# A mixture stage's routing: 64 squares on ACT for four subtractions on POOL, and the shares' operations at an earlier place

## The reference

```python
gate_logits = jnp.einsum('ble,en->bln', x, gate_kernel)
top_k_weights, top_k_indices = jax.lax.top_k(gate_logits, TOP_K)
softmax_probs = jax.nn.softmax(top_k_weights.astype(jnp.float32), axis=-1)
weights = weights.at[b_idx, l_idx, top_k_indices].set(softmax_probs)
layer_w0 = jnp.einsum('ble,neh->blnh', x, w0_kernel)
layer_w1 = jnp.einsum('ble,neh->blnh', x, w1_kernel)
layer_mult = jax.nn.silu(layer_w0) * layer_w1
intermediate = jnp.einsum('blnh,nhe->blne', layer_mult, wo_kernel)
output = jnp.einsum('blne,bln->ble', intermediate, weights)
```

## Time and profile before

| | before |
|---|---|
| median of 3 runs | 2676.36 us |
| the profiled execution: its time | 2678.13 us |
| the profiled execution: its span | 2676.4 us |
| routing, first operation on DVE to last | 2195.24 to 2233.45 us |
| first gather of the block loop | 2235.35 us |
| start of the last scatter | 2664.57 us |

### The profile page before, as it was taken

One profiled execution on the slowest core, in us unless ns is written; L12 is line 12 of the kernel. 1 busy time (PEld: TensorE's weight loads), 2 busy tenths in 40 slices (PEclk: granted clock), 3 DMA queues, 4 the chain that ended last, 5 costly groups with the idle time before them and its releaser, 6 DMA issues. The chain is left out here.

```text
span 2676.4 us, 42235 instructions
## 1 busy us (share of the span) xinstructions
PE 2422.9 (91%) x12786; PEld 1425.6 (53%) x12787; DVE 1609.7 (60%) x3262; ACT 1287.1 (48%) x2560; POOL 1317.3 (49%) x2110
## 2 busy tenths in 40 slices
PE   6997999999996895899999999899969975999997
PEld 3554666766663563344445354356546663666664
DVE  5885664755554984787877778488867654121211
ACT  4664443534442792466666566566653421222221
POOL 3665664234435663323443435466875315666663
PEclk9998999999998997899999999899989987999999
DMA  4001000000100005122231231100004151222222
GB/s 139 6 1 64 4 0 0 1 1 1 40 8 16 1 1 124 27 61 67 51 93 43 62 81 37 48 24 25 1 1 166 48 199 27 46 44 47 45 46 28
DMA packets 85456, 115.24 MB, mean 43 GB/s; under 512 B 15432, under 2 KB 64433, under 8 KB 83601
## 3 DMA queue, kind: packets, MB, share of 16 engines
q1 hardware_dynamic: 66736, 92.36, 11.5%
q0 software_dynamic: 18528, 20.50, 4.8%
HBM read 77.92 MB, written 34.64 MB: 42 GB/s over the span
## 5 line engine op out<-in xcount | busy, mean ns | idle before, releaser
L3415 ACT ACTIVATE L2S_pT<-L2S_t_ps 128x512 f32<-128x512 f32 (+3 forms) x768 | 356.3, 491 | 218.4 <-PE L2S_t_ps L3239 210.1
L3479 DVE TENSOR_REDUCE L2S_mx<-L2S_s_ps 128x1 f32<-128x768 f32 (+7 forms) x384 | 350.7, 951 | 114.6 <-PE L2S_s_ps L3162 114.0
L3239 PE MATMUL L2S_t_ps<-L2S_q,L2S_k 98*128 98x512 bf16 (+3 forms) x768 | 249.9, 336 | 17.6 <-DMA L2S_q<-L2S_mrow 6.6
L3719 POOL TENSOR_SCALAR_AFFINE_SELECT L2S_pT<-L2S_pT 128x128 f32<-128x128 f32 x512 | 152.2, 312 | 175.1 <-ACT L2S_pT L3415 170.5
L3161 PE MATMUL L2S_s_ps<-L2S_k,L2S_q 96*128 96x512 bf16 (+3 forms) x768 | 200.3, 333 | 17.5 <-DMA L2S_q<-qk_parts 9.0
L622 POOL TENSOR_TENSOR L_prob<-L_prob,L_rc 128x616 f32<-128x616 f32 x64 | 82.4, 1287 | 231.3 <-DVE L_rc L555 231.3
L4095 DVE TENSOR_TENSOR L3B_h<-L3B_si,L3B_u_ps 128x512 f32<-128x512 f32 x71 | 48.8, 688 | 237.3 <-PE L3B_u_ps L4038 234.5
L4012 POOL DMA_INDIRECT out<-L3B_y,L3F_rows x71 | 114.8, 1617 | 132.4 <-DVE L3B_y L4101 119.9
L3239 PEld LDWEIGHTS L2S_t_ps<-L2S_q,L2S_k 98*128 98x128 bf16 x768 | 73.3, 98 | 197.7 <-ACT L2S_pT L3415 128.7
L3339 PE MATMUL L2S_o_ps<-L2S_pT,L2S_v 128*32 128x512 f32 (+3 forms) x1536 | 165.8, 505 | 0.0
L319 PE MATMUL L_scores<-weights,L_xT 128*128 128x308 f32 x512 | 143.1, 423 | 2.3 <-ACT L_xT L442 1.6
(11 more groups left out here) (542 smaller groups left out, 5765.5 us busy)
## 6 DMA issues: line engine op xcount, KB each, us to landing
qk_parts<-L2S_part SPq DMA_DIRECT2D x90, 128.0 KB, 2.4
L2S_q<-qk_parts SPq DMA_DIRECT2D x32, 192.0 KB, 3.4
L2S_k<-qk_parts SPq DMA_DIRECT2D x30, 192.0 KB, 3.4
L2S_q<-qk_parts SPq DMA_DIRECT2D x32, 128.0 KB, 3.2
L3F_w<-in_L_gu SPq DMA_DIRECT2D x8, 512.0 KB, 7.3
weights<-in_L_w SPq DMA_DIRECT2D x8, 512.0 KB, 9.7
out<-x_sb SPq DMA_DIRECT2D x8, 512.0 KB, 4.1
expert_rows<-L_xn SPq DMA_DIRECT2D x8, 512.0 KB, 3.2
```

What stands on the lines that cost most here:

```text
L3239: nc.tensor.matmul(o[:, lo:512], k6[:, q % 2, j, kt * P:(kt + 1) * P], q6[:, q % 2, c, j, lo:512], start=True, stop=True).then_inc(s["t_fu ...
L3415: nc.scalar.activation(pT[:, st % SLOTS, j, lo:512], t_ps[j % 2][:, lo:512], ACT.Exp, scale=SK).then_inc(s["exp_done"], 1)
L3479: nc.vector.tensor_reduce(dst, src, AX.X, ALU.max).then_inc(s["mx_done"], 1)
L3719: nc.gpsimd.affine_select(out=edge, in_=edge, compare_op=ALU.is_ge, fill=0.0, base=0, pattern=[[1, P]], channel_multiplier=-1).then_inc(s[ ...
```

## The change

In `place_tokens` the four subtractions on POOL go. ACT makes `lines` instead, after its copy of the shares, by 64 activations of 128x72 with the function Square: each takes `jota` as input and a column of `line` as bias. So that the bias is the negative line, L3917 multiplies by -1/P. A square is zero where the difference is, and `weigh` asks only for that. Every 16th square counts on `spot_done`. The four operations on the shares move on DVE from behind `spread(0)` to ahead of its wait for `placed`.

In `expert_blocks` the gathers of the shares get semaphores of their own, `shared[j % 4]`. TensorE's `turn_x` waits for the rows alone, DVE's `result` waits for the shares, and POOL waits, before the gather of block j, for the share gather of block j - 4. ACT begins the part with a Silu of one column into a tile `ready`, which nobody reads.

```diff
--- before.py
+++ after.py
@@ -3874,6 +3874,12 @@
             nc.scalar.activation(share[:, 1, :], share[:, 1, :], ACT.Exp).then_inc(s["ratio_done"], 1)
             act.wait_ge(s["shareT_full"], 1)
             nc.scalar.activation(shareT[:], sT_ps[0:PAIRS, 0:P], ACT.Copy).then_inc(s["shareT_done"], 1)
+            act.wait_ge(s["line_done"], 1)
+            chip.settle(act)
+            for n in range(PAIRS):
+                ins = nc.scalar.activation(lines[:, n, :], a["jota"][:], ACT.Square, bias=line[:, n:n + 1], scale=1.0)
+                if n % PART == PART - 1:
+                    ins.then_inc(s["spot_done"], 1)
 
         @block.vector
         def _(dve):
@@ -3900,6 +3906,12 @@
             nc.vector.tensor_tensor(share[:, 1, :], top[:, 1, :], top[:, 0, :], ALU.subtract).then_inc(s["share_raw"], 1)
             link(nc.vector.tensor_tensor(tri8[:], wide(chip.iota[:, 0:E].unsqueeze(2), [P, E, E]), wide(chip.iota[:, 0:E].unsqueeze(1), [P, E, E]), ALU.is_ge))
 
+            dve.wait_ge(s["ratio_done"], 1)
+            link(nc.vector.tensor_scalar(share[:, 0, :], share[:, 1, :], 1.0, None, ALU.add))
+            link(nc.vector.reciprocal(share[:, 0, :], share[:, 0, :]))
+            link(nc.vector.tensor_tensor(share[:, 1, :], share[:, 0, :], share[:, 1, :], ALU.mult))
+            nc.vector.tensor_scalar(share[:].rearrange("p k t -> p (k t)"), share[:].rearrange("p k t -> p (k t)"), 1.0, chip.gates[:, B + 3:B + 4],
+                                    ALU.mult, ALU.mult).then_inc(s["share_done"], 1)
             dve.wait_ge(s["placed"], 1)
             link(nc.vector.tensor_tensor(over[:], wide(c_ps[:, TE:TE + E].unsqueeze(2), [P, E, T]), wide(a["steps"][:].unsqueeze(1), [P, E, T]), ALU.is_gt))
             link(nc.vector.tensor_reduce(blocks[:], over[:], AX.X, ALU.add))
@@ -3914,7 +3926,7 @@
             link(nc.vector.tensor_scalar(sloti[:], sloti[:], P - 1, None, ALU.bitwise_and))
             link(nc.vector.tensor_copy(spot[:], sloti[:]))
             link(nc.vector.tensor_tensor(line[:], slot[:], spot[:], ALU.subtract))
-            nc.vector.tensor_scalar(line[:], line[:], 1.0 / P, None, ALU.mult).then_inc(s["line_done"], 1)
+            nc.vector.tensor_scalar(line[:], line[:], -1.0 / P, None, ALU.mult).then_inc(s["line_done"], 1)
 
             def spread(c):
                 part = slice(c * PART, (c + 1) * PART)
@@ -3929,12 +3941,6 @@
                                                op0=ALU.is_equal, op1=ALU.mult).then_inc(s["lines_done"], 1)
 
             spread(0)
-            dve.wait_ge(s["ratio_done"], 1)
-            link(nc.vector.tensor_scalar(share[:, 0, :], share[:, 1, :], 1.0, None, ALU.add))
-            link(nc.vector.reciprocal(share[:, 0, :], share[:, 0, :]))
-            link(nc.vector.tensor_tensor(share[:, 1, :], share[:, 0, :], share[:, 1, :], ALU.mult))
-            nc.vector.tensor_scalar(share[:].rearrange("p k t -> p (k t)"), share[:].rearrange("p k t -> p (k t)"), 1.0, chip.gates[:, B + 3:B + 4],
-                                    ALU.mult, ALU.mult).then_inc(s["share_done"], 1)
             weigh(0)
             for c in range(1, PAIRS // PART):
                 spread(c)
@@ -3955,15 +3961,6 @@
             link(nc.vector.tensor_scalar(rowf[:, 2, :], token[:], 0.0, None, ALU.max))
             nc.vector.tensor_copy(a["rows"][:], rowf[:])
 
-        @block.gpsimd
-        def _(pool):
-            pool.wait_ge(s["line_done"], 1)
-            chip.settle(pool)
-            for c in range(PAIRS // PART):
-                part = slice(c * PART, (c + 1) * PART)
-                nc.gpsimd.tensor_tensor(lines[:, part, :], wide(a["jota"][:].unsqueeze(1), [P, PART, NJ]), wide(line[:, part].unsqueeze(2), [P, PART, NJ]),
-                                        ALU.subtract).then_inc(s["spot_done"], 1)
-
 
 def expert_blocks(chip, dram, a):
 
@@ -3987,6 +3984,7 @@
         names = "xT_full xT_free g_full u_full si_done h_done hT_full hT_free o_full y_done".split()
         s = {n: ctx.enter_context(nc.semaphore(f"L3B_{n}")) for n in names}
         loaded, added = [chip.queued[f"gathered{q}"] for q in range(AHEAD)], chip.queued["scattered0"]
+        shared, ready = [chip.queued[f"gathered{AHEAD + q}"] for q in range(AHEAD)], sb("ready", [P, 1])
         block = ctx.enter_context(nc.Block())
         none = lambda j, q: None
 
@@ -3998,11 +3996,12 @@
             def gather(j):
                 if j >= AHEAD:
                     pool.wait_ge(s["xT_full"], j - AHEAD + 1)
+                    pool.wait_ge(shared[j % AHEAD], 16 * (j // AHEAD))
                     chip.settle(pool)
                 nc.gpsimd.indirect_dma_start(xb[:, j % AHEAD, :], None, dram["rows"], bass.IndirectOffsetOnAxis(rows[:, 0, j:j + 1], 0)
                                              ).then_inc(loaded[j % AHEAD], 16)
                 nc.gpsimd.indirect_dma_start(share[:, j % (2 * AHEAD):j % (2 * AHEAD) + 1], None, dram["shares"],
-                                             bass.IndirectOffsetOnAxis(rows[:, 2, j:j + 1], 0)).then_inc(loaded[j % AHEAD], 16)
+                                             bass.IndirectOffsetOnAxis(rows[:, 2, j:j + 1], 0)).then_inc(shared[j % AHEAD], 16)
 
             def scatter(j):
                 pool.wait_ge(s["y_done"], j + 3)
@@ -4022,7 +4021,7 @@
         @block.tensor
         def _(pe):
             def turn_x(j, q):
-                pe.wait_ge(loaded[q % AHEAD], (j - q) * (32 // AHEAD) + 32 * (q // AHEAD) + 32)
+                pe.wait_ge(loaded[q % AHEAD], (j - q) * (16 // AHEAD) + 16 * (q // AHEAD) + 16)
                 pe.wait_ge(s["xT_free"], j + 1)
                 for k in range(KD):
                     mm = nc.tensor.transpose(xT_ps[:, k * P:(k + 1) * P], xb[:, q % AHEAD, k * P:(k + 1) * P], chip.ident[:])
@@ -4060,6 +4059,7 @@
         def _(act):
             act.sem_inc(s["xT_free"], 1)
             act.sem_inc(s["hT_free"], 1)
+            nc.scalar.activation(ready[:], chip.neghalf[:, 0:1], ACT.Silu)
 
             def copy_x(j, q):
                 act.wait_ge(s["xT_full"], j + 1)
@@ -4098,6 +4098,7 @@
                 dve.wait_ge(s["o_full"], j + 1)
                 if not (isinstance(j, int) and j < AHEAD):
                     dve.wait_ge(added, (j - AHEAD + 1) * 16)
+                dve.wait_ge(shared[q % AHEAD], (j - q) * (16 // AHEAD) + 16 * (q // AHEAD) + 16)
                 nc.vector.tensor_scalar(y[:, q % AHEAD, :], o_ps[q % 2][:, 0:D], share[:, q:q + 1], None, ALU.mult).then_inc(s["y_done"], 1)
 
             run(dve, [none, none, mul, none, result, none])
```

## The result

The changed kernel takes 2671.22 us (median of 16 runs), the kernel before 2675.61 us, measured beside it (16 runs). The ratio is 0.9984, its 95% interval 0.9977 to 0.9992: 4.4 us, or 0.16%, faster. The forecast was 5.07 us and 2671.3. The profiled execution has a span of 2670.5 us against 2676.4.

What follows compares the result with a forecast made beforehand. The routing was bound by a DVE and POOL chain, the block loop by TensorE. Terms -4.24 (squares, +0.15 contained), -0.9 (turn of x), 0 (Silu), +0.07 (waits) sum to -5.07: 2671.3 us, range 2668.3 to 2674.8 with rivals.

Steps and rivals of the forecast that it cites:

- The squares: Routing: 64 ACT squares replace POOL's subtractions and set the pace, L3942 at 2224.94 instead of 2229.18, -4.24 us, +0.15 contained.
- neighbours overlap: Routing, ACT: successive squares overlap, so they start 0.250 us apart, though one alone takes 350 ns.
- a pace by DVE: Routing rival: squares under 0.21 us leave DVE as the limit, -8.0 us there, -8.8 in all, 2667.5; 9 in 100.
- Shares ahead of the wait: Routing, DVE: the shares' four operations mostly fit a 0.88 us hole before `placed`, delaying L3904 by 0.15 us.
- The 6.17 us on the path are gone: Routing, DVE: moving the shares' four operations, stretched beside POOL, takes their 6.17 us off the path.
- The turn of x: Loop start: with own share semaphores, TensorE's turn of block 1 waits for rows alone, 2240.75 instead of 2241.64, -0.9 us.
- all after it is a full TensorE: Block loop: `g` stands behind the turn of x, then TensorE is fully busy; the loop takes over start shifts unchanged.
- a rise at another distance from the first product: Loop start, sign of a wrong forecast: TensorE's clock rises at another distance from the first product than before.
- the start gives nothing: Loop start rival: the rows' receipt ends last anyway, so only -4.2 us in all, 2672.2; 13 in 100.
- The early Silu: Block loop's entry: the 1.28 us table load moves before the first gather has landed, worth 0; at worst some 0.3 us.
- The waits in the loop: Block loop: new DVE wait before each `y`, only the last counts, +0.07 us; rival, on the path, slower: 5 in 100.
- A table for Square: Routing rival: a table load for Square behind the wait for `line` adds 1.28 us, -3.8 in all, 2672.6; 5 in 100.

Runs made afterwards that it cites:

- e3: Kernel before with only the shares' four operations moved ahead of the wait for `placed`; one run, table's first operation at 28.48 us instead of 28.56.
- e5: Changed kernel with the shares' operations back behind DVE's first comparison and ACT's share copy behind its squares; one run, table's first operation at 23.86 us against 24.08.
- e4: Changed kernel with the first quarter's 16 squares given back to POOL as one addition; one run, table's first operation at 22.74 us against 24.08.
- e1: Kernel before with the new `place_tokens` only, the old `expert_blocks` kept; ratio to before 0.9984 (0.9972 to 0.9995).
- e6: Kernel before with POOL's four subtractions cut into 16 of 4 columns; one run, table's first operation at 29.51 us instead of 28.56.
- e2: Kernel before with the new `expert_blocks` only, the old routing kept; ratio to before 0.9997 (0.9986 to 1.0008).
- e7: Changed kernel with the first quarter's 16 squares given back to POOL as one addition, timed; ratio to before 0.9979 (0.9970 to 0.9988).
- e11: Changed kernel without the early Silu at the block loop's entry; one run, last scatter at 458.99 us against 459.46.
- e12: The changed kernel measured again, unedited, as a control; ratio to before 0.9983 (0.9971 to 0.9994).
- e10: Changed kernel without the gathers of the shares, `y` multiplied by 0.5 instead; one run, TensorE's second turn 4.27 us after the first gather instead of 5.50.
- e9: e7 plus 52 unread TensorE transposes: 10 behind the routing's last product, 28 at loop entry, 14 behind the first turn; ratio to before 0.9967 (0.9956 to 0.9978).
- e8: e7 plus 22 unread TensorE transposes: 10 behind the routing's last product, 12 at loop entry; ratio to before 0.9976 (0.9967 to 0.9985).

## Why the prediction was right

**The total.** Forecast -5.07, measured -4.4 (0.9984; the interval is -6.2 to -2.1 us), in the pair of traces -4.49 at the last scatter. The time lay in the range, within 0.2%, as the likelier side had it. What carries it is the term of the squares, 4.24 of the 5.07, and that was right as to its mechanism. That the total came out so near is in part luck: in the first pair the start's 0.9 came to nothing at the last scatter, and the squares gave 0.24 more than was forecast.

**The squares: -4.24, measured -4.48.** The step "neighbours overlap", with 0.250 from start to start, held at 0.246; the ranges' ends of 0.30 and of a pace by DVE are excluded. ACT sets the pace, DVE's waits show it. The estimate of 0.247 from the figures of the Trainium skill ("ScalarE: Activation LUTs", section "What ACT_TABLE_LOAD costs") is 0.001 off.

**Shares ahead of the wait: +0.15, measured +0.24 at L3916 and 0.21 at `line`.** Right in sign, and the size was off since DVE started 0.12 us after the end of Exp (0.06 was taken), and the gaps between the linked operations were a little longer.

**"The 6.17 us on the path are gone": the step that failed.** It was no term of the sum by itself, since I took the difference of two whole chains, but it is wrong as a reason. e3 takes those four operations off and gains 0.08 (0.30 from the line on). e5 leaves them on and gains as much as the change and 0.22 more. The 10.21 us on POOL were said to "leave no hole that counts" behind them; in truth POOL's four subtractions, at 2.11 us alone, were 8.4 us of the path, because DVE's instructions wait for their ends. Leaving them out gives 28.56 - 22.74 + 2.24 = 8.06 us, had DVE never to wait (e4's table operation has 2.00 of waiting and the 0.24 of the shares in it). ACT's pace takes 1.99 + 3 x 0.36 of that, the shares' place 0.24, and some 0.10 more go at each of the last three waits (a quarter takes 3.93, where the round is 3.47 and the idle time 0.36): 3.6 in all. What is left is 4.5.

**The turn of x: -0.9, measured -0.88 and then nothing to -0.6 at the fourth block.** Over the profiles the second turn is at 6.29 to 6.45 with the old semaphores (before, e1, e3, e6: mean 6.38) and at 5.46 to 5.58 with the new (changed, e2, e4, e5, e7, e11, e12: mean 5.49). That part is shown. The step "all after it is a full TensorE" holds only half. In the groups with the late copy, the fourth block's g is at 23.28 to 23.47 with either. In the others it is at 23.00 and 23.90 with the old, mean 23.45, and at 22.26 to 23.29 with the new, mean 22.85: -0.6, with a scatter of that same size. The scatter comes from the clock, which the sum didn't have: the rise came 2.68 to 6.11 us behind the first g in kernels that don't differ there. Since a microsecond ahead of the rise counts half, a start 0.9 earlier is worth 0.45 if the rise doesn't come along with it and 0.9 if it does (an estimate from the 3.72 plus half the rise above); the profiles are too few to say which. The prediction named a rise at another distance from the first product as a sign that it was wrong, and it did come: 2.68 instead of 4.42. It was worth 0.87 in the first pair and was lost again behind the late copy. The rival "the start gives nothing" was right in the first profile and is neither shown nor excluded in the mean; e2's ratio of 0.9997 can't tell it.

**The early Silu: 0, measured 0** (e11).

**The waits in the loop: +0.07, not seen.** The period is 5.82 us in both kernels and POOL idles about 1.64 us ahead of a scatter in both, so that rival is out. From the fourth block's g to the last scatter it is 405.80 to 405.97 us with the old semaphores and 405.74 to 405.96 with the new (e10 left out), so a term of 0.07 can't be told from none.

**A table for Square:** no load stands before the squares; out.

## What to carry to other kernels

Where DVE and POOL work side by side and a small DVE operation takes ten times its length, as here, ask first whether it waits for one of POOL's instructions to end; POOL's instructions cut small show it (e6). If so, count both engines' lengths into one sum, and look for a third engine to take POOL's part; moving the stretched operation away gave 0.08 us here. If an engine then waits for the first piece in any case, that is a place where POOL's instruction is free (e4). Where a loop that TensorE bounds starts after a stage in which TensorE was idle, look at the granted clock under its first products: it was 0.50 (1.2 GHz) here. Filling the gap up to the first real product brought the fourth block's g 2 to 3 us forward in the one profile of e9, against the others with the new semaphores and without the late copy (e10 aside); filling a part of it (e8) brought nothing.

## What the runs showed that I had not expected

- DVE and POOL exclude each other by whole instructions in these rows, but for the reciprocal. An operation of 0.18 us took 2.09 beside subtractions of 2.11 and 0.64 beside pieces of a quarter of that. The same work in another order has the same end to 0.08 us (28.56 and 28.48).
- TensorE's granted clock was lost over two idle stretches of 2.28 and 2.06 us with one turn of x between them (e8: 12 transposes in 1.50 us before them, a product of four in 3.78 after them), and was kept where there was none (e9: 1.98).
- The time from the first g to the second varies by 1.7 us (5.07 to 6.77) between executions in which nothing differs there, as half of the time to the clock's rise. An effect of half a microsecond behind it can't be read from one profile.
- ACT's first copy of h comes 19.57 to 19.68 us after the first gather in all profiles of two groups, and 14.5 to 18.1 us after it, with TensorE's turn of h, in all profiles of the two others. POOL's eighth gather is late with it. None of the edits of e5 to e8 moved it, and I don't know what it waits for; the chip differed with it, where it is on record.
